# Attention heads of a fused float32 block: sixteen units turn their second head's probabilities on VectorE and through HBM, and use them a step later

## The chip, the cores and the metric

The kernel runs as one program on one core of a Trainium2 chip. The metric is the device time of one execution in microseconds (us), as the median of several runs. A profiled execution of the same program gives the trace from which all rows below are taken.

## What is computed

The reference is one layer on 512 tokens of width 1024, all in float32:

```python
x = x + cross_attention(layernorm(x), ctx, mask)      # 8192 context rows, width 1024
x = x + self_attention(layernorm(x))                  # 16 heads of 64, 4 key/value heads
x = x + expert_ffn(layernorm(x))                      # 16 experts, top 2, and a shared part
```

The change is nearly all in the second line. For each group of heads it computes, with causal masking, RMS-normed and rotated q and k:

```python
scores = einsum('bkgtd,bksd->bkgts', qg, k) * scale
attn = softmax(where(causal, scores, -inf), axis=-1)
y = einsum('bkgts,bksd->bkgtd', attn, v)
y_out = y - sum(y * vn) * vn                          # vn: v at unit length
out = y_out @ Wproj + y_out @ p_A @ p_B
```

## The kernel before

**Stages.** Layer norm and projections of the cross-attention come first, then the loop over the context in 8 pairs of chunks, then the self-attention, then the experts. Large products are made of three passes each (high times high, low times high, high times low), which are the matmuls of lines 37, 38 and 39. In the trace's names `banks` is PSUM.

**The loop over the context.** A pair of chunks has 7 products of two tiles each (`product`), whose scores VectorE takes with the mask (`scored`, line 1693, and `hold`, line 1676). ScalarE's `exps` makes the probabilities, VectorE's `turn` (line 1709) transposes each 32x32 block of them, SyncE stores the tile to HBM (`store_turned`, line 800) and fetches it back in four DMAs with the blocks in their places (`load_turned`, line 808), and ScalarE and VectorE split it into a high and a low part (`pt_hi`, line 1381, and `pt_lo`). `keys_hi` and `keys_lo` split the keys. Each engine's order is written out by hand; the change touches `first_half`, that of the first pair. There TensorE may begin the product numbered 3 when `added` has reached 3, which is the first `hold`, and its second tile at 4, which is the second `hold`.

**The self-attention.** There are 32 units: a tile of 128 queries and a pair of heads. Units 0 to 7 see 512 keys, 8 to 15 see 384, 16 to 23 see 256 and 24 to 31 see 128. A step `st` of the loop does on each engine, in this order:

- TensorE: the scores of unit st (line 1205), the transposes of the probabilities of unit st-1, both heads (line 1218), the values of unit st-2 (line 1234), and in between parts of the projections of later pieces (`fill`, lines 37 to 39), which have nothing to do with these units. At some half steps (`slot`) it also turns a piece or a row of outputs.
- ScalarE: at some steps the copy of a projected piece (line 1533); the copy of the first head's transposed probabilities of unit st-1 out of PSUM (`pt_act`, line 1568), then the exponentials of unit st (`exps`, line 1577), then at some steps squares of a piece; a turned piece is copied at its slot (line 1561).
- VectorE: causal mask and row maxima of unit st (lines 1930 and 1934), the copy of the second head's transposed probabilities of unit st-1 (`pt_dve`, line 1942), `row_recip`, the taking of the values of unit st-2 (line 1952), and work on the pieces.
- GpSimd: small products of the outputs, and DMAs: the output weights (`load_output_weights`, line 952), tables.
- SyncE: before the loop's first step it has issued `clear_rows` (line 778), one DMA of zeros into `y_dram`, and then it waits until all pieces are turned, to load the first shared expert weights (line 884).

`s_exp`, `pt_ready`, `pt_act`, `pt_dve`, `y_ready` and `y_done` count these operations; a buffer of transposed probabilities, `pT_sb`, holds two units.

Of the kernel before, what the change touches and what calls it, by code (L numbers as in the profile page):

```python
# [7 lines left out]
F32 = mybir.dt.float32  # L8
# [3 lines left out]
ACT = mybir.ActivationFunctionType  # L12
AX = mybir.AxisListType

P = 128
# [4 lines left out]
W = 512  # L20
# [500 lines left out]
H, HKV, HD = 16, 4, 64  # L521
# [14 lines left out]
HALVES_SPLIT = 15  # L536
TILE_OF = (2, 3, 0, 1, 0, 1, 2, 3)
PT_RING = 8
Y_BANK, FILL_BANK = 4, 5
MINC = 10  # L540
MAXC = (2 * T - 16) // P + 16
# [23 lines left out]
def attention(nc, block, m, ins, resid, QT, K, V, X, raw, PT, at, in_loaded, raw_loaded, ident, y_cleared, ln, d, F, weff,  # L565
# [28 lines left out]
    with ExitStack() as stage:  # L594
# [162 lines left out]
        def keys_of(u):  # L757
            return (SEQ[u // PAIRS] + 1) * P

        def s_banks(u):  # L760
            return bank[:, 2:4, :] if u % 2 == 0 else bank[:, 6:8, :]

# [19 lines left out]
        def _(sp):  # L782
# [29 lines left out]
            def pair_of_chunks(s_):  # L812
# [74 lines left out]
        def _(pool):  # L887
# [115 lines left out]
            root(6)  # L1003
            turn_by_sin(6)
            for st in range(3, UNITS + 4):
                if st % 2 == 0 and st >= 4:
                    part_along((st - 4) // 2)
                if st % 2 and (st - 3) // 2 < 4 * HKV:
                    times_value((st - 3) // 2)
# [23 lines left out]
        def _(pe):  # L1033
# [175 lines left out]
            def heads_transpose(u):  # L1209
                pe.wait_ge(s["s_exp"], u + 1)  # L1210
                if u >= 1:
                    pe.wait_ge(s["pt_act"], u)
                    pe.wait_ge(s["pt_dve"], u)
# [8 lines left out]
            def heads_values(u):  # L1222
                g = 2 * (u % PAIRS) // GROUP
                pe.wait_ge(s["pt_act"], u + 1)
                pe.wait_ge(s["pt_dve"], u + 1)
                if u == 0:
                    pe.wait_ge(s["piece_copied"], AHEAD)
                k = 2 * (u + 2)
                if not slot_read(pe, k) and not slot_read(pe, k - 1) and u >= 1:
                    pe.wait_ge(s["y_done"], u)  # L1230
                keys = keys_of(u) // P
                for h in range(2):
                    for k in range(keys):
                        mm = pe.matmul(bank[:, Y_BANK, h * HD:(h + 1) * HD],  # L1234
                                       pT_sb[:, u % 2, h, k * P:(k + 1) * P], v_sb[:, k, g * HD:(g + 1) * HD],
                                       start=k == 0, stop=k == keys - 1)
                mm.then_inc(s["y_ready"], 1)

# [9 lines left out]
            def slot(k):  # L1248

                if k not in PIECE_SLOTS.values() and k not in ROWS_SLOTS.values():  # L1250
                    return
                step = k // 2
                if k % 2 or not slot_read(pe, k - 1):
                    if step - 1 - (k % 2 == 0) >= 1:
                        pe.wait_ge(s["y_done"], step - 1 - (k % 2 == 0))
# [91 lines left out]
        def _(act):  # L1347
# [61 lines left out]
            def first_half():  # L1409
                keys_hi(2)  # L1410
                keys_hi(3)
                copy_first(0, 0)
                copy_first(0, 1)
                keys_hi(4)
                keys_hi(5)
                exps(0)
                keys_hi(6)
                exps(1)
                keys_hi(7)
                keys_hi(8)  # L1420
                keys_hi(9)
                pt_hi(0)
# [140 lines left out]
            def pt_act(u):  # L1563
                n = keys_of(u)
                act.wait_ge(s["pt_ready"], u + 1)
                if u >= 2:
                    act.wait_ge(s["y_ready"], u - 1)
                act.activation(pT_sb[:, u % 2, 0, 0:n], bank[:, 0, 0:n], ACT.Copy).then_inc(s["pt_act"], 1)

            def exps(u):  # L1570
                n = keys_of(u)
                act.wait_ge(s["s_max"], u + 1)
                if u >= 2:
                    act.wait_ge(s["pt_ready"], u - 1)
                    act.wait_ge(s["recip_done"], u - 1)
                for h in range(2):
                    op = act.activation(p_sb[:, u % 2, h, 0:n], s_banks(u)[:, h, 0:n], ACT.Exp,
                                        bias=s_neg_max[:, u % 2, h:h + 1], accum_out=s_rowsum[:, u % 2, h:h + 1])
                op.then_inc(s["s_exp"], 1)

# [74 lines left out]
        def _(dve):  # L1655
# [117 lines left out]
            def first_half():  # L1773
# [163 lines left out]
            def pt_dve(u):  # L1937
                n = keys_of(u)
                dve.wait_ge(s["pt_ready"], u + 1)
                if u >= 2:  # L1940
                    dve.wait_ge(s["y_ready"], u - 1)
                dve.tensor_copy(pT_sb[:, u % 2, 1, 0:n], bank[:, 1, 0:n]).then_inc(s["pt_dve"], 1)

            def row_recip(u):
                dve.wait_ge(s["s_exp"], u + 1)
# [96 lines left out]
            for st in range(UNITS + 2):  # L2042
                if st >= OUT_STEP + 3 and (st - OUT_STEP) % 3 == 0:
                    add_out((st - OUT_STEP - 3) // 3)
                slot(2 * st)
                if st < UNITS:
                    maxima(st)
                if 1 <= st <= UNITS:
                    pt_dve(st - 1)
                    row_recip(st - 1)  # L2050
                if st >= 2:
                    take_y(st - 2)
                if st >= 4 and st % 2 == 0:
                    dot((st - 4) // 2)
                if st >= 5 and st % 2 == 1:
                    take_along((st - 5) // 2)
                slot(2 * st + 1)
                if st == 0:
                    turn_by_cos(5)
# [1100 lines left out]
```

## Time and profile before

| | |
|---|---|
| median of 3 runs | 1351.06 us (1350.43 to 1351.42) |
| the profiled execution's own time | 1351.05 us |
| span of its trace | 1349.3 us |
| TensorE busy | 1326.9 us (98%) |
| VectorE, ScalarE busy | 927.6 us (69%), 719.2 us (53%) |

The span is the stretch from the first to the last instruction; 1.75 us of the execution's own time lie around it. Busy time of an engine is the union of its instructions; a matmul's end is modelled, so the length of a piece of TensorE's work is better read from start to start. In rows of the trace PE is TensorE, PEld its weight loads, DVE VectorE, ACT ScalarE, POOL GpSimd, SP SyncE.

### The profile page before, as it was taken

What the parts mean: (1) busy time and instruction counts of PE and PEld (TensorE: products, weight loads), DVE (VectorE), ACT (ScalarE), POOL (GpSimd) and SP (SyncE); (2) the same over time, 40 slices, a digit from 0 to 9 for tenths busy, and PEclk for the clock granted to TensorE, in tenths of its full rate; (3) what the DMA queues carried; (4) which work ended last, traced back from release to release, by engine and by line L of the source; (5) the groups of instructions that cost most, each with busy time, mean ns of one, the idle gap of its engine ahead of it and who ended that gap; (6) DMA issues with size and microseconds to landing.
All of it is one profiled execution on the core that took longest, in us unless ns stands there. A gap on an engine that the chain in (4) does not pass through costs nothing.

```text
span 1349.3 us, 17583 instructions
## 1 busy us (share of the span) xinstructions
PE 1326.9 (98%) x6228; PEld 1087.2 (81%) x6228; DVE 927.6 (69%) x1416; ACT 719.2 (53%) x1165; POOL 184.4 (14%) x244
## 2 busy tenths in 40 slices
PE   7999999999999999999999999999999999999999
PEld 5878878888888888888888888777777888888887
DVE  6757867675775857667675775867666676767665
ACT  3333446574665656656565653655433345667561
POOL 3000100000000000000000000634331022122113
PEclk9999999999999999999999999999999999999999
DMA  7457274674746748465575445503403357988676
GB/s 249 155 216 249 83 240 158 213 231 141 249 137 214 220 138 282 126 214 176 196 225 164 142 140 196 171 1 125 148 14 114 136 187 254 305 299 306 224 250 218
DMA packets 102887, 253.25 MB, mean 188 GB/s; under 512 B 10080, under 2 KB 56224, under 8 KB 89440
## 3 DMA queue, kind: packets, MB, share of 16 engines
q1 hardware_dynamic: 89136, 192.97, 43.6%
q0 software_dynamic: 10784, 48.93, 10.6%
q10 hardware_dynamic: 2880, 10.22, 1.9%
q8 instruction: 50, 0.82, 0.2%
q14 instruction: 37, 0.30, 0.1%
HBM read 210.67 MB, written 41.42 MB: 187 GB/s over the span
## 4 chain that ended last, share of the span: by engine, by line
PE 93%; DVE 3%; issue 1%; ACT 1%; DMA 1%; POOL 1%; SPq 0%; POOLq 0%; DVEq 0%; ACTq 0%
PE banks L37 25%; PE banks L39 25%; PE banks L38 25%; PE a_banks L37 3%; PE a_banks L38 3%; PE a_banks L39 3%; PE banks L1234 3%; PE banks L1205 2%; PE banks L1218 2%; DMA e_raw<-w_down 1%; PE banks L2444 1%; DVE e_lo L2778 0%; POOL c_ms L933 0%; DVE QT_lo L1873 0%; PE a_banks L273 0%
## 5 line engine op out<-in xcount | busy, mean ns | idle before, releaser
L37 PE MATMUL banks<-V_hi,b_PT_hi 128*128 128x512 f32 x512 | 199.3, 389 | 0.0
L38 PE MATMUL banks<-V_lo,b_PT_hi 128*128 128x512 f32 x512 | 199.2, 389 | 0.0
L39 PE MATMUL banks<-V_hi,b_PT_lo 128*128 128x512 f32 x512 | 199.2, 389 | 0.0
L1392 ACT ACTIVATE resid<-banks 128x1024 f32<-128x1024 f32 x64 | 65.5, 1023 | 104.0 <-PE banks L39 104.0
L2778 DVE TENSOR_TENSOR e_lo<-e_raw,e_hi 128x1024 fp32r<-128x1024 f32 x80 | 96.1, 1242 | 34.8 <-ACT e_hi L2605 34.1
L37 PEld LDWEIGHTS banks<-V_hi,b_PT_hi 128*128 128x128 f32 x512 | 96.1, 188 | 20.1 <-DVE V_lo L1663 0.2
L39 PEld LDWEIGHTS banks<-V_hi,b_PT_lo 128*128 128x128 f32 x512 | 96.1, 188 | 19.9
L38 PEld LDWEIGHTS banks<-V_lo,b_PT_hi 128*128 128x128 f32 x512 | 96.1, 188 | 19.9
L1693 DVE CUSTOM_DVE_ANT_0 b_s<-banks,b_s,b_row_max 128x512 f32<-128x512 f32 x60 | 45.0, 751 | 85.6 <-PE banks L39 85.6
L890 POOL DMA_DIRECT2D b_s<-mask x32 | 23.2, 726 | 575.8 <-DVE b_turned L1709 550.1
L37 PE MATMUL banks<-b_k_hi,QT_hi 128*128 128x512 f32 x256 | 99.6, 389 | 0.0
L38 PE MATMUL banks<-b_k_lo,QT_hi 128*128 128x512 f32 x256 | 99.6, 389 | 0.0
L39 PE MATMUL banks<-b_k_hi,QT_lo 128*128 128x512 f32 x256 | 99.6, 389 | 0.0
L2605 ACT ACTIVATE e_hi<-e_raw 128x1024 fp32r<-128x1024 f32 x80 | 81.7, 1061 | 29.2 <-DMA e_raw<-w_down 20.0
L1363 ACT ACTIVATE b_k_hi<-b_k_raw 128x1024 fp32r<-128x1024 f32 x60 | 61.6, 1049 | 38.8 <-DVE b_k_raw L1745 20.5
L37 PE MATMUL banks<-b_k_hi,b_q_hi 128*128 128x512 f32 x192 | 75.5, 393 | 2.5 <-DVE b_s L1676 2.5
L1658 DVE TENSOR_TENSOR b_k_lo<-b_k_raw,b_k_hi 128x1024 fp32r<-128x1024 f32 x60 | 71.7, 1220 | 5.5 <-ACT b_k_hi L1363 5.5
L39 PE MATMUL banks<-b_k_hi,b_q_lo 128*128 128x512 f32 x192 | 75.3, 392 | 0.0
L38 PE MATMUL banks<-b_k_lo,b_q_hi 128*128 128x512 f32 x192 | 75.3, 392 | 0.0
L1676 DVE TENSOR_TENSOR b_s<-banks,b_s 128x512 f32<-128x512 f32 x32 | 22.0, 691 | 77.1 <-PE banks L39 77.1
L1663 DVE TENSOR_TENSOR V_lo<-b_v_raw,V_hi 128x2048 fp32r<-128x2048 f32 x30 | 68.7, 2289 | 3.5 <-ACT V_hi L1372 3.5
L1398 ACT ACTIVATE banks<-resid,b_alpha 128x1024 f32<-128x1024 f32 x60 | 67.2, 1120 | 2.0
(364 smaller groups left out, 3236.7 us busy)
## 6 DMA issues: line engine op xcount, KB each, us to landing
b_v_raw<-kv SPq DMA_DIRECT2D x30, 1024.0 KB, 5.6
e_raw<-w_up SPq DMA_DIRECT2D x40, 512.0 KB, 5.2
e_raw<-w_down SPq DMA_DIRECT2D x40, 512.0 KB, 6.3
b_k_raw<-kv SPq DMA_DIRECT2D x19, 1024.0 KB, 5.5
raw<-kv SPq DMA_DIRECT2D x18, 1024.0 KB, 5.5
b_s<-mask POOLq DMA_DIRECT2D x32, 512.0 KB, 5.8
pt_dram<-b_turned SPq DMA_DIRECT2D x64, 256.0 KB, 3.3
b_p_in<-pt_dram SPq DMA_DIRECT2D x256, 64.0 KB, 4.2
```

Source lines behind the costliest of these rows:

```text
L37: pe.matmul(out, lhs_hi, rhs_hi, start=first, stop=False, skip_group_check=onto)
L38: pe.matmul(out, lhs_hi, rhs_lo, start=False, stop=False, skip_group_check=onto)
L39: return pe.matmul(out, lhs_lo, rhs_hi, start=False, stop=last, skip_group_check=onto)
L1234: mm = pe.matmul(bank[:, Y_BANK, h * HD:(h + 1) * HD], pT_sb[:, u % 2, h, k * P:(k + 1) * P], v_sb[:, k, g * HD:(g + 1) * HD], start=k == ...
L1363: act.activation(k_hi[:, j % 3, :, :], keys_raw(j), ACT.Copy).then_inc(hi_done, 1)
L1392: act.activation(resid[:, TILE_OF[n % PER_PAIR], :], O_ps(n), ACT.Copy).then_inc(b["acc_done"], 1)
L1398: act.activation(O_ps(n), resid[:, TILE_OF[c], :], ACT.Copy, scale=alpha[:, c:c + 1]).then_inc(b["seeded"], 1)
L1658: dve.tensor_tensor(k_lo[:, j % 3, :, :], keys_raw(j), f32(k_hi[:, j % 3, :, :]), ALU.subtract).then_inc(split_done, 1)
L1663: dve.tensor_tensor(value_slot(V_lo, vh), v_raw[:, :, :], f32(value_slot(V_hi, vh)), ALU.subtract).then_inc(b["v_split"], 1)
L1693: dve.tensor_tensor_reduce(slot, score_bank(s_, i, t), slot, 1.0, LEAST if n < TB else top_before, ALU.add, ALU.max, top).then_inc(b["adde ...
L2605: act.activation(e_hi(first + j), e_raw[:, j, :], ACT.Copy).then_inc(s["e_hi"], 1)
L2778: dve.tensor_tensor(e_lo[:, first + j, :], e_raw[:, j, :], f32(e_hi(first + j)), ALU.subtract).then_inc(s["e_split"], 1)
```

## The change

Units 0 to 15 (`MOVED`) no longer have their second head transposed on TensorE. `exps` writes that head's probabilities with their 32-column blocks in another order, VectorE transposes 32x32 blocks (`turn_probs`), SyncE stores the tile to HBM, waits for it and fetches it in four DMAs (`move_probs`), and ScalarE copies it into order (`keep_moved`). The values of these units are computed at step u+3 instead of u+2 (`LATE`), so step 18 has the values of units 15 and 16. What follows from the values (`take_y`, `times_value`, `dot`, `part_along`, `take_along`) follows a step later too, and two turns of output rows are moved from half steps 40 and 42 to 42 and 44. The loop's `clear_rows` comes behind the sixteen moves on SyncE. In the first pair of chunks `exps(1)` goes ahead of `keys_hi(6)`, `turn(0)` ahead of `keys_lo(6)`, and `hold(0, 0, 0)` ahead of `keys_lo(7)`.

```diff
+MOVED = 2 * PAIRS
+LATE = 1
-ROWS_SLOTS = {8: 28, 9: 30, 10: 40, 11: 42, 12: 56, 13: 58}
+ROWS_SLOTS = {8: 28, 9: 30, 10: 42, 11: 44, 12: 56, 13: 58}
+        p_turned, p_moved, p_kept = (at(f"c_p_{x}", [P, 2, W], F32, "raw", 4096 * i)
+                                      for i, x in enumerate(("turned", "moved", "kept")))
...
+        def kept(u, h):
+            return pT_sb[:, u % 4 // 2, u % 2, :] if u < MOVED else pT_sb[:, u % 2, h, :]
+        def values_at(st):
+            early = [st - 2 - LATE] if 0 <= st - 2 - LATE < MOVED else []
+            return early + ([st - 2] if MOVED <= st - 2 < UNITS else [])
...
@@ sync
+            def move_probs(u):
+                n, done = keys_of(u), STEPS // 2 + u // 2
+                sp.wait_ge(b["turned"], STEPS + u + 1)
+                sp.dma_start(pt_dram[u % PT_RING][:, 0:n], p_turned[:, u % 2, 0:n]).then_inc(b[f"pt_stored{u % 2}"], 16)
+                sp.wait_ge(b[f"pt_stored{u % 2}"], 16 * (done + 1))
+                if u >= 2:
+                    sp.wait_ge(b["pt_hi"], STEPS + u - 1)
+                for j in range(4):
+                    sp.dma_start(p_moved[32 * j:32 * j + 32, u % 2, 0:n].rearrange("p (a r) -> p a r", a=4),
+                                 pt_dram[u % PT_RING][:, 0:n].rearrange("(a i) (b r) -> b i a r", a=4, b=4)[j]
+                                 ).then_inc(pt_loaded[u % 2], 16)
...
+            for u in range(MOVED):
+                move_probs(u)
             clear_rows(sp)
@@ tensor
-                for h in range(2):
+                for h in range(1 if u < MOVED else 2):
                     for k in range(keys_of(u) // P):
                         mm = pe.transpose(bank[:, h, k * P:(k + 1) * P],
...
-                if st >= 2:
-                    heads_values(st - 2)
+                for u in values_at(st)[:1]:
+                    heads_values(u, st)
                 fill(st, 0)
+                for u in values_at(st)[1:]:
+                    heads_values(u, st)
@@ scalar, first_half
                 exps(0)
+                exps(1)
                 keys_hi(6)
-                exps(1)
@@ scalar
+            def keep_moved(u):
+                act.wait_ge(pt_loaded[u % 2], (16 if u % 2 == 0 else 0) + 64 * (STEPS // 2 + u // 2 + 1))
...
+                if 0 <= st - 2 - LATE < MOVED:
+                    keep_moved(st - 2 - LATE)
                 if 1 <= st <= UNITS:
                     pt_act(st - 1)
@@ vector, first_half
                 scored(1)
+                turn(0)
                 keys_lo(6)
-                turn(0)
-                keys_lo(7)
                 turn(1)
                 hold(0, 0, 0)
+                keys_lo(7)
                 hold(0, 0, 1)
@@ vector
+            def turn_probs(u):
+                dve.wait_ge(s["s_exp"], u + 1)
...
+                dve.transpose(p_turned[:, u % 2, 0:n], p_sb[:, u % 2, 1, 0:n]).then_inc(b["turned"], 1)
...
+                if 1 <= st <= MOVED:
+                    turn_probs(st - 1)
                 if st < UNITS:
                     maxima(st)
+                if MOVED < st <= UNITS:
+                    pt_dve(st - 1)
```

## Rows read from the trace of the kernel before

**Rows 1.** TensorE's wait in the first pair: us in total, times, longest.

```profile
PE banks L37 <- DVE b_s L1676: 2.5, 1, 2.5
```

**Rows 2.** Windows: length, busy us (instructions) of PE, PEld, DVE, ACT, POOL; clock; DMA share, GB/s.

```profile
864.60:908.00 43.40, 43.34 (x263) 32.17 (x263) 32.42 (x61) 24.01 (x93) 17.93 (x18) 1.00 0.00 1
908.00:948.00 40.00, 40.00 (x262) 31.06 (x261) 29.93 (x63) 21.28 (x79) 17.64 (x22) 1.00 0.28 106
```

**Rows 3.** Timeline of TensorE, a step with 512 keys, one with 384: start, us.

```profile
895.68 1.13 PE L1205 MATMUL banks<-c_kT,c_qT 64*128 64x512 f32 x4
896.74 1.09 PE L1218 MATMUL banks<-ident,c_probs 128*128 128x128 f32 x8
897.67 1.90 PE L1234 MATMUL banks<-c_v,c_PT 128*128 128x64 f32 x16
...
914.38 0.88 PE L1218 MATMUL banks<-ident,c_probs 128*128 128x128 f32 x6
915.09 1.90 PE L1234 MATMUL banks<-c_v,c_PT 128*128 128x64 f32 x16
```

**Rows 4.** The lines of block transpose, of copies; ns min/median/max, first and last start.

```profile
L1709 DVE STREAM_TRANSPOSE b_turned<-b_s x64: 702/703/710, 168.2 to 781.8; 128x512 f32<-128x512 f32 x64
...
L1942 DVE COPY c_PT<-banks x32: 280/482/681, 870.8 to 1012.1; 128x512 f32<-128x512 f32 x8, 128x384 f32<-128x384 f32 x8, 128x256 f32<-128x256 f32 x8, 128x128 f32<-128x128 f32 x8
...
L1381 ACT ACTIVATE b_PT_hi<-b_p_in x64: 611/616/635, 176.9 to 799.1; 128x512 fp32r<-128x512 f32 x64
```

**Rows 5.** Timeline of the second exponential of a 512-key and of a 384-key unit.

```profile
899.83 0.20 ACT L1577 ACTIVATION_READ_ACCUMULATOR c_probs<-banks,c_neg_max 128x1 f32 x1
...
916.99 0.20 ACT L1577 ACTIVATION_READ_ACCUMULATOR c_probs<-banks,c_neg_max 128x1 f32 x1
```

**Rows 6.** Timeline of SyncE's queue, first stores and loads of turned tiles.

```profile
168.90 2.12 SPq L800 DMA_DIRECT2D pt_dram<-b_turned  x2
171.06 3.85 SPq L808 DMA_DIRECT2D b_p_in<-pt_dram  x8
```

**Rows 7.** The page's DMA issues: KB each, median us to landing.

```profile
pt_dram<-b_turned SPq DMA_DIRECT2D x64, 256.0 KB, 3.3
b_p_in<-pt_dram SPq DMA_DIRECT2D x256, 64.0 KB, 4.2
```

**Rows 8.** Timeline, second and third step of the heads, VectorE, ScalarE, TensorE.

```profile
868.36 0.69 DVE L1888 TENSOR_TENSOR c_cosp<-c_piece,c_cos 128x512 f32<-128x512 f32 x1
...
873.73 0.43 DVE L1930 TENSOR_TENSOR banks<-banks,c_causal 128x256 f32<-128x256 f32 x1
...
875.45 0.69 ACT L1577 ACTIVATE c_probs<-banks,c_neg_max 128x512 f32<-128x512 f32 x1 [0.51 <-DVE c_neg_max L1934]
...
875.82 0.19 PEld L37 LDWEIGHTS banks<-K_hi,QT_hi 128*128 128x128 f32 x1
...
877.62 1.13 PE L1205 MATMUL banks<-c_kT,c_qT 64*128 64x512 f32 x4
877.72 0.60 ACT L1561 ACTIVATE c_qT<-banks 128x512 f32<-128x512 f32 x1 [0.83 <-PE banks L1163]
...
878.22 0.59 ACT L1533 ACTIVATE c_piece<-banks 128x512 f32<-128x512 f32 x1
```

**Rows 9.** A window behind the first pair's wait (columns as in rows 2).

```profile
173.00:174.00 1.00, 1.00 (x4) 0.81 (x3) 0.02 (x1) 0.00 (x0) 0.00 (x0) 0.50 0.83 168
```

**Rows 10.** Timeline of the first pair, ahead of that wait's end.

```profile
166.89 0.71 ACT L1406 ACTIVATE b_s<-b_s,b_neg_max 128x512 f32<-128x512 f32 x1
...
167.02 1.23 DVE L1658 TENSOR_TENSOR b_k_lo<-raw,b_k_hi 128x1024 fp32r<-128x1024 f32 x1 [0.88 <-ACT b_k_hi L1363]
...
170.61 1.28 DVE L1676 TENSOR_TENSOR b_s<-banks,b_s 128x512 f32<-128x512 f32 x2
```

**Rows 11.** Landings in the heads' stretch, and the zeros over the span.

```profile
K_lo<-weff_lo POOLq DMA_DIRECT2D x4, 1024.0 KB, 9.9
...
y_dram<-c_zeros SPq DMA_DIRECT2D x1, 6656.0 KB, 27.7
```

More of the change, by code:

```diff
@@ L758, in keys_of, with by_lanes, kept_free, values_through @@
             return (SEQ[u // PAIRS] + 1) * P
+        def by_lanes(x, n):
+            return x.rearrange("p (b k i) -> p k b i", b=4, k=n // P)
+        def kept(u, h):
+            return pT_sb[:, u % 4 // 2, u % 2, :] if u < MOVED else pT_sb[:, u % 2, h, :]
+        def kept_free(eng, u, h):
+            if u < MOVED:
+                if u >= 4:
+                    eng.wait_ge(s["y_ready"], u - 3)
+            elif u < MOVED + 2:
+                eng.wait_ge(s["y_ready"], MOVED - 3 + 2 * (u % 2) + h)
+            else:
+                eng.wait_ge(s["y_ready"], u - 1)
+        def values_at(st):
+            early = [st - 2 - LATE] if 0 <= st - 2 - LATE < MOVED else []
+            return early + ([st - 2] if MOVED <= st - 2 < UNITS else [])
+        def values_through(st):
+            return sum(len(values_at(i)) for i in range(st + 1))
+        def late_group(st, after):
+            q, odd = divmod(st - after - LATE, 2)
+            early = [q] if not odd and 0 <= q < MOVED // 2 else []
+            q, odd = divmod(st - after, 2)
+            return early + ([q] if not odd and MOVED // 2 <= q < UNITS // 2 else [])
         def s_banks(u):
@@ L1005, in _ @@
             for st in range(3, UNITS + 4):
[L1006 to L1009, printed above, removed]
+                for q in late_group(st, 4):
+                    part_along(q)
+                for q in late_group(st, 3):
+                    times_value(q)
                 if st in TAKEN:
@@ L1220, in heads_transpose, with heads_values @@
                 mm.then_inc(s["pt_ready"], 1)
-            def heads_values(u):
+            def heads_values(u, st):
                 g = 2 * (u % PAIRS) // GROUP
                 pe.wait_ge(s["pt_act"], u + 1)
-                pe.wait_ge(s["pt_dve"], u + 1)
+                if u < MOVED:
+                    pe.wait_ge(b["pt_hi"], STEPS + u + 1)
+                else:
+                    pe.wait_ge(s["pt_dve"], u - MOVED + 1)
                 if u == 0:
                     pe.wait_ge(s["piece_copied"], AHEAD)
-                k = 2 * (u + 2)
-                if not slot_read(pe, k) and not slot_read(pe, k - 1) and u >= 1:
+                k = 2 * st
+                if values_at(st)[0] != u:
+                    pe.wait_ge(s["y_done"], u)
+                elif not slot_read(pe, k) and not slot_read(pe, k - 1) and u >= 1:
                     pe.wait_ge(s["y_done"], u)
@@ L1233, in heads_values @@
                     for k in range(keys):
-                        mm = pe.matmul(bank[:, Y_BANK, h * HD:(h + 1) * HD],
-                                       pT_sb[:, u % 2, h, k * P:(k + 1) * P], v_sb[:, k, g * HD:(g + 1) * HD],
+                        if u < MOVED and h:
+                            left = p_kept[:, u % 2, k * P:(k + 1) * P]
+                        else:
+                            left = kept(u, h)[:, k * P:(k + 1) * P]
+                        mm = pe.matmul(bank[:, Y_BANK, h * HD:(h + 1) * HD], left, v_sb[:, k, g * HD:(g + 1) * HD],
                                        start=k == 0, stop=k == keys - 1)
@@ L1253, in slot @@
                 if k % 2 or not slot_read(pe, k - 1):
-                    if step - 1 - (k % 2 == 0) >= 1:
-                        pe.wait_ge(s["y_done"], step - 1 - (k % 2 == 0))
+                    if values_through(step - (k % 2 == 0)) >= 1:
+                        pe.wait_ge(s["y_done"], values_through(step - (k % 2 == 0)))
                 for i, at_slot in PIECE_SLOTS.items():
@@ L1565, in pt_act @@
                 act.wait_ge(s["pt_ready"], u + 1)
+                kept_free(act, u, 0)
+                act.activation(kept(u, 0)[:, 0:n], bank[:, 0, 0:n], ACT.Copy).then_inc(s["pt_act"], 1)
+            def keep_moved(u):
+                n = keys_of(u)
+                act.wait_ge(pt_loaded[u % 2], (16 if u % 2 == 0 else 0) + 64 * (STEPS // 2 + u // 2 + 1))
                 if u >= 2:
                     act.wait_ge(s["y_ready"], u - 1)
-                act.activation(pT_sb[:, u % 2, 0, 0:n], bank[:, 0, 0:n], ACT.Copy).then_inc(s["pt_act"], 1)
+                act.activation(p_kept[:, u % 2, 0:n].rearrange("p (k a j) -> p k a j", a=4, k=n // P),
+                               p_moved[:, u % 2, 0:n].rearrange("p (a k j) -> p k a j", a=4, k=n // P),
+                               ACT.Copy).then_inc(b["pt_hi"], 1)
             def exps(u):
@@ L1575, in exps @@
                     act.wait_ge(s["recip_done"], u - 1)
+                if 2 <= u < MOVED + 2:
+                    act.wait_ge(b["turned"], STEPS + u - 1)
                 for h in range(2):
-                    op = act.activation(p_sb[:, u % 2, h, 0:n], s_banks(u)[:, h, 0:n], ACT.Exp,
+                    to, of = p_sb[:, u % 2, h, 0:n], s_banks(u)[:, h, 0:n]
+                    if u < MOVED and h:
+                        to, of = by_lanes(to, n), of.rearrange("p (k b i) -> p k b i", b=4, k=n // P)
+                    op = act.activation(to, of, ACT.Exp,
                                         bias=s_neg_max[:, u % 2, h:h + 1], accum_out=s_rowsum[:, u % 2, h:h + 1])
@@ L1939, in pt_dve @@
                 dve.wait_ge(s["pt_ready"], u + 1)
+                kept_free(dve, u, 1)
+                dve.tensor_copy(kept(u, 1)[:, 0:n], bank[:, 1, 0:n]).then_inc(s["pt_dve"], 1)
+            def turn_probs(u):
+                n = keys_of(u)
+                dve.wait_ge(s["s_exp"], u + 1)
                 if u >= 2:
-                    dve.wait_ge(s["y_ready"], u - 1)
-                dve.tensor_copy(pT_sb[:, u % 2, 1, 0:n], bank[:, 1, 0:n]).then_inc(s["pt_dve"], 1)
+                    dve.wait_ge(b[f"pt_stored{u % 2}"], 16 * (STEPS // 2 + u // 2))
+                else:
+                    dve.wait_ge(s["w_split"], 6)
+                dve.transpose(p_turned[:, u % 2, 0:n], p_sb[:, u % 2, 1, 0:n]).then_inc(b["turned"], 1)
             def row_recip(u):
@@ L2045, in _ @@
                 slot(2 * st)
+                if 1 <= st <= MOVED:
+                    turn_probs(st - 1)
                 if st < UNITS:
                     maxima(st)
+                if MOVED < st <= UNITS:
+                    pt_dve(st - 1)
                 if 1 <= st <= UNITS:
-                    pt_dve(st - 1)
                     row_recip(st - 1)
[L2051 to L2056, printed above, removed]
+                for u in values_at(st):
+                    take_y(u)
+                for q in late_group(st, 4):
+                    dot(q)
+                for q in late_group(st, 5):
+                    take_along(q)
                 slot(2 * st + 1)
```

3 lines of the change are left out of this document (2 added, 1 removed).

## Prediction

> **What bounds the kernel now.** I read the busy shares first: TensorE is at work in 98% of the span, every other engine in 69% or less. The windows of the heads' stretch came next [rows 2]: TensorE is busy for 43.34 of 43.40 us while the units with 512 keys run, and for all of the 40.00 us of those with 384, at a granted clock of 1.00, the 2.4 GHz level. So a transpose taken off TensorE shortens this stretch, as long as nothing else takes its place. VectorE has 32.42 and 29.93 us of work there, ScalarE 24.01 and 21.28. The list of TensorE's waits gave the one place in the loop over the context where it stands still, 2.5 us for a `hold` in the first pair of chunks [rows 1]; behind it the clock falls to 0.50, the 1.2 GHz level [rows 9]. The timelines of the engines gave the rest.
>
> **The transposes.** From the first transpose to the first value matmul it is 897.67 - 896.74 = 0.93 us for eight, and 915.09 - 914.38 = 0.71 us for six [rows 3], so 0.11 us for each one more. Eight units lose four each (8 x 0.44 = 3.5 us) and eight lose three (8 x 0.33 = 2.6 us): **-6.2 us**. If each were worth its mean, 0.93 / 8 = 0.116, the 56 would give 6.5 us. The fill between is the same work.
>
> The Trainium skill, VectorE: DVE Perf Modes, section "Rules for kernel authors", speaks against the change: for a full 128x128 transpose it names TensorE where PSUM is an acceptable destination. That rule weighs one transpose by itself; in this trace VectorE's block transpose of 128x512 takes 0.703 us [rows 4], against 0.44 us of TensorE saved, and what decides is that TensorE is the full engine.
>
> **VectorE and ScalarE.** For the copy out of PSUM, 0.681 us at most, VectorE gets a block transpose of 0.703 us [rows 4]: nothing. ScalarE gets the copy into order as one more operation: the same kind of permuted copy takes 0.616 us [rows 4], 16 x 0.6 = 10 us in 83 us in which it is idle for 38. It covers this itself; what counts is where it stands, since `pt_act` and the next `exps` are queued behind its wait for the DMAs.
>
> **The round trip.** Scores of a 512-key unit start at 895.68 and its exponentials end at 900.03 [rows 3, 5], 4.35 us later. Turn, 0.70 us: 5.05. Then SyncE: a store issued at 168.90 has landed by the first load at 171.06, and the four loads are 1.9 us of issuing; the copy that waits for them begins at 176.9 [rows 4, 6], 8.0 us after the store. That gives 13.1 us, and 13.7 with ScalarE's copy. The values need it three steps later behind scores and transposes. A step is 43.4 / 8 = 5.4 us now [rows 2] and about 5.0 then: 15.0 + 1.06 + 0.5 = 16.5 us. Slack 2.8 us. With 384 keys: the last exponential of the unit whose transposes follow at 914.38 ends at 917.19 [rows 5], 3.7 us after its scores began 0.85 us ahead of those transposes; 0.5 + 8.0 + 0.5 more are 12.7 us, against 3 x 4.7 + 1.2 = 15.3. Slack 2.6 us. Where VectorE has 2 us of a piece's work ahead of the turn, about 0.6 is left. SyncE is busy with a unit for 2.16 + 1.9 = 4.1 us, less than a step. Its added waits, for the turn, the landing and `keep_moved` of unit u-2, hold up nothing but its own next units and the zeros; `exps(u)` also waits for the turn of unit u-2, which is a step old by then. The DMA engines are as good as idle until 908 us (0.00) [rows 2]. So in the quiet steps: nothing.
>
> **The start.** The values of unit 0 no longer fill step 2, while the first units' exponentials take as long as before. VectorE ends the piece's product at 869.05 [rows 8], turns unit 0 until 869.75, and comes to the maxima of unit 2 at 873.8 as before, but with a turn of 0.70 first: 874.5. From the mask to the exponentials it is 875.45 - 873.73 = 1.7 us [rows 8], and they take 1.45: 877.65. TensorE's transposes of unit 1 begin at 873.2 now (the fill behind them at 875.82 [rows 8], less 0.93 for them and 1.7 for the values) and at about 873.0 then, held by that unit's exponentials, until 873.5; then fill and a piece's turn, 877.62 - 875.82 = 1.8 us [rows 8], then scores, 1.06: 876.35. It waits 1.4 us for the exponentials of unit 2, transposes until 878.2, and then wants `keep_moved(0)`. ScalarE has a turned piece (0.5) and a piece's copy (0.6) ahead of it: 877.65 + 0.5 + 0.6 + 0.6 = 879.4. That is 1.2 us more: **+2.6 us**. The value work left out is done at step 18. Bounds: 1 us, if ScalarE's two copies come after or overlap, 4 if maxima slip once more or the clock falls.
>
> **Output weights and zeros.** GpSimd's 4 MB of output weights, twice, take about 10 us each until the last has landed [rows 11]. The first falls on about three moves of units 10 to 13. No row shows a move beside just these. Below: nothing. By the medians of the loop over the context, 3.3 and 4.2 us [rows 7] against 2.0 to 2.2 and some 3.5, a unit loses 2 us, of which its slack of 0.6 to 2.6 covers most, and SyncE falls 1.3 us behind a unit with 0.6 spare in each step: a stall of 0 to 2 us. I take **+0.6**, nearer to the quiet rows, since only one transfer competes; above, 4 us.
>
> The Trainium skill, DMA: Bandwidth & Descriptors, section "Queues, rings and completion order", has each DMA engine change between queues only after a whole packet of one; by this the small transfers wait behind the weights' packets, but a few, not the whole 4 MB. No row of this kernel shows it alone, and the term above doesn't use it.
>
> The zeros, 27.7 us long [rows 11], now start behind unit 15, at about 945 us, together with the second output weights. Those are needed some 12 us later, and 20 for the second half. Sharing may delay them by 0 to 4 us, most of it covered; **+0.2**. The shared weights land behind the zeros some 15 us later than now, and are first read after 1010.
>
> **The first pair.** With `exps(1)` (0.9 us) first, the key half that TensorE needs is split 1.1 us later: `keys_lo(6)` from 168.1 to 169.3 instead of 167.02 [rows 10], then a turn until 170.0 and the first `hold` until 170.6; today the two holds are at 170.61 to 171.89 [rows 10]. TensorE starts 0.65 us earlier, but its second tile wants the second `hold`, now behind `keys_lo(7)`, at 172.4: 0.45 us back. **-0.2 us**. The bounds: +0.5, and -2.4 if the shorter stretch of rest leaves the clock up: behind today's, some 3.4 us run at the 1.2 GHz level [rows 9], worth 1.7.
>
> **Sum.** -6.2 - 0.2 + 2.6 + 0.6 + 0.2 = -3.0 us, made against the profiled execution's 1351.05 us, which is the median of the runs to 0.01: **1348.1 us**.
>
> **Rivals.**
> 1. *The whole gain arrives.* The start's waits are covered, and the first pair keeps its clock: 1351.05 - 6.2 - 1.9 + 1.0 = 1344.0. For it: two of my terms are worked out to tenths from instruction starts. Against: no work is left to TensorE in step 2.
> 2. *Little is left.* The clock falls at the start, where TensorE now rests 2.6 us within 3.1, much as in the first pair: +1.7, or the weights cost 2 us more: 1349.5 to 1350. For it: rows 9. Against: the rest is in two pieces with transposes between.
> 3. *The move is too slow, and it ends slower.* SyncE takes the units one by one, so store, its landing and four issues bound the step. It decides from 4.7 us on. At the median landing of 3.3 us it is 3.3 + 0.1 + 1.9 = 5.3 us, over eight steps of 5.0 and eight of 4.7: 2.4 + 4.8 = 7.2 us lost: 1348.1 + 7.2 = 1355.3. For it: the median is of the same transfer. Against: that median has megabyte loads ahead in the same queue, and the heads' stretch has none.
>
> **Chances.** Forecast 0.43, little left 0.27, whole gain 0.13, too slow 0.17. 0.2% is 2.7 us, about what a measurement of this kernel can tell from no change, so the line lies at 1348.4, and the forecast case straddles it: faster 0.50 (0.37 of the forecast and the whole gain), same 0.31, slower 0.19. The likeliest case's own range is 1346.5 to 1349.3; over all cases 1343.8 to 1354.5.
>
> **What would show it.** TensorE waits of 1.4 and 1.2 us for the exponentials of unit 2 and for `keep_moved(0)`; 104 transposes in line 1218's place instead of 160; ScalarE's `keep_moved` seldom waiting for a DMA except at units 10 to 13; steps of about 5.0 and 4.7 us; the same 83 us of work 3 us shorter in all; in the first pair two waits of 1.8 and 0.4 us. Landings above 3 us in the quiet steps, or a wait of TensorE for ScalarE in every step, would make it wrong.

## The result, and the profile after

The changed kernel takes 1367.77 us (median of 4 runs, 1366.31 to 1369.51) against 1350.74 us of the kernel before (4 runs, 1348.37 to 1351.42): ratio 1.0132, interval 1.012 to 1.0144. It is 17 us slower, on the other side of no change and outside the range. The profiled execution took 1366.4 us, of which 1364.6 are span: 15.35 us over the profiled execution of before.

The sum of the forecast must have missed something of about 18 us, and something so large is seen in the list of TensorE's waits. Of the kernel after (us in total, times, longest):

```profile
PE banks L1292 <- ACT c_p_kept L1633: 7.7, 2, 6.8
PE banks L1292 <- issue: 5.9, 1, 5.9
PE banks L1292 <- DVE QT_lo L1947: 2.2, 5, 0.7
...
PE banks L37 <- DVE b_s L1750: 1.6, 1, 1.6
PE banks L1267 <- ACT c_probs L1649: 1.3, 1, 1.3
```

Line 1292 is the values (1234 before), line 1633 `keep_moved`, line 1267 the transposes. The value matmuls stand still twice, for 6.8 and 5.9 us; in the same list of before the values wait 0.7 us at most. The two waits forecast for the start are there too: 1.3 us for the exponentials, and 7.7 - 6.8 = 0.9 us for `keep_moved(0)`. The windows of the kernel after say where (columns as in rows 2). These go from the scores of unit 0 to those of units 8, 13 and 14, and on over the second place:

```profile
862.43:903.52 41.09, 38.92 (x220) 27.36 (x220) 31.38 (x60) 26.98 (x98) 17.19 (x18) 1.00 0.28 90
903.52:928.65 25.13, 25.13 (x158) 19.03 (x157) 18.21 (x39) 15.07 (x57) 11.65 (x15) 1.00 0.43 145
928.65:943.08 14.43, 7.63 (x30) 5.86 (x29) 3.98 (x8) 3.51 (x16) 3.93 (x5) 0.69 0.65 214
943.08:960.82 17.74, 17.56 (x111) 13.04 (x110) 11.89 (x28) 12.14 (x44) 5.47 (x9) 0.97 0.40 125
960.82:975.00 14.18, 8.32 (x35) 7.20 (x36) 1.82 (x6) 1.71 (x7) 2.58 (x3) 0.64 1.10 369
```

Until 928.65 all is about as forecast. Then step 13 takes 14.43 us where a step takes 4.6, and another 5.9 us are lost behind 960.82. In both places the clock is below 1.00. What TensorE waits for at 930.04 is read in the chain that ended last, of the kernel after (start, us):

```profile
920.76 1.86 DMA pt_dram<-c_p_turned
922.64 0.30 SPq L898
...
924.49 11.70 DMA c_p_moved<-pt_dram
936.22 0.53 ACT c_p_kept L1633
936.84 2.80 PE banks L1292 x12
```

The store of unit 10 lands in 1.86 us, its four loads in 11.70. What else was on its way shows only in GpSimd's own timeline of the kernel after, which the chain doesn't name:

```profile
921.46 0.64 POOL L1000 DMA_DIRECT2D K_hi<-weff_hi  x1
922.11 0.55 POOL L1000 DMA_DIRECT2D K_lo<-weff_lo  x1
922.65 0.54 POOL L1000 DMA_DIRECT2D K_hi<-weff_hi  x1
923.18 0.54 POOL L1000 DMA_DIRECT2D K_lo<-weff_lo  x1
```

These are the output weights, 1 MB each, issued just before and between the four loads of 48 KB. By the trace the weights landed at 926.8, 929.6, 932.5 and 935.9, and the loads, issued from 922.64 to 924.49, at 930.0, 932.9, 935.4 and 936.2. That looks like one line in order of issue, in which a load waits for all weights issued before it. But the third load, issued at 923.91, behind the last of the weights, landed half a microsecond before that one. The packets of the two queues, the pieces in which the DMA engines move a transfer, tell what happened. These are GpSimd's queue (q0) and SyncE's (q1) of the kernel after, from 924 to 927 us and from 927 to 930 (packets, MB, share of the 16 DMA engines' time):

```profile
q0 software_dynamic: 161, 1.19, 102.9%
q1 hardware_dynamic: 23, 0.01, 1.8%
```

```profile
q0 software_dynamic: 145, 1.06, 92.9%
q1 hardware_dynamic: 148, 0.05, 10.5%
```

From 927 us on the two queues alternate, one packet of the weights for one of the loads, and from 930 to 933 it is 145 and 143. The weights' packets carry 8 KB, the loads' 384 bytes. The eight megabytes of the output weights are 1152 packets, so 144 for each: 128 with data and 16 of a few bytes that end it. The four loads of unit 11, quiet ones, and the start of a store, from 937 to 939.5 us:

```profile
DMA packets 667, 0.34 MB, mean 135 GB/s; under 512 B 576, under 2 KB 667, under 8 KB 667
```

576 packets for four loads are 144 for each of 48 KB, as many as a megabyte of weights has. So while weights are under way, a load takes as long as a megabyte: 144 of its packets at 148 in 3 us are 2.9 us, and the second landed 2.9 us behind the first. Before that, from 922.7 to 926.4 us, SyncE's queue moved 4 packets and GpSimd's 173, though in a quiet step a load has landed after 2.0 us. What held the loads back there no run shows.

The second place is much the same with unit 15, whose loads are issued from 956.02 and the second four megabytes from 955.87: 156 packets of the weights and 158 of SyncE's queue from 961 to 964 us. Two summaries of the tile `c_p_moved` after show how rare this is, and so why a median says nothing of it:

```profile
L1633 ACT ACTIVATE c_p_kept<-c_p_moved x16: 514/572/645, 876.0 to 967.3; 128x512 f32<-128x512 f32 x8, 128x384 f32<-128x384 f32 x8
...
  DMA c_p_moved<-pt_dram: 12.5, 2
...
DMA to landing us min/median/max: 1.7/2.0/11.7
```

The stop costs more than its length. These windows of the kernel after take in the work from the end of either wait, 936.84 and 967.90, to where the clock comes back, and one of the work between the two places:

```profile
967.90:974.90 7.00, 7.00 (x27) 6.42 (x28) 0.68 (x3) 1.08 (x5) 0.73 (x1) 0.50 1.11 345
936.84:944.20 7.36, 7.36 (x26) 5.73 (x26) 2.89 (x6) 2.41 (x7) 2.52 (x3) 0.50 0.32 80
944.30:962.04 17.74, 17.56 (x114) 13.18 (x112) 11.92 (x30) 11.13 (x42) 6.08 (x10) 1.00 0.48 153
```

At 0.50, the 1.2 GHz level, 7.36 and 7.00 us of work would have been half as long: 3.7 and 3.5 us more lost.

**The account of the traces.** Two waits, 6.80 + 5.86 = 12.7 us; the clock behind them, 7.2; two waits at the start, 2.2; transposes, -6.2 as forecast. That is 15.9 us, and the two traces show 17.1 from the scores of unit 0 to those of unit 31 (1023.59 - 862.43 = 161.16 us after, 1008.71 - 864.66 = 144.05 before), so 1.2 us of the transposes' gain did not come. The scores of unit 0 themselves start 2.2 us earlier, and what follows unit 31 adds 0.4: 17.1 - 2.2 + 0.4 = 15.3.

### The profile page after: what moved, and what is told of

It reads as the page before. It is cut to its first block, busy times and chain, and to the rows that moved or that the text cites. A ratio compares the mean times of both kernels' runs of the same rounds, so it can differ in the third digit from the quotient of the medians.

```text
span 1364.6 us, 17612 instructions
## 1 busy us (share of the span) xinstructions
PE 1328.6 (97%) x6172; PEld 1086.8 (80%) x6172; DVE 925.7 (68%) x1416; ACT 726.4 (53%) x1181; POOL 185.7 (14%) x244
## 4 chain that ended last, share of the span: by engine, by line
PE 91%; DVE 3%; issue 2%; DMA 1%; POOL 1%; ACT 1%; SPq 0%; ACTq 0%; POOLq 0%; DVEq 0%
PE banks L37 25%; PE banks L39 24%; PE banks L38 24%; PE a_banks L37 3%; PE a_banks L38 3%; PE a_banks L39 3%; PE banks L1292 3%; PE banks L1253 1%; DMA c_p_moved<-pt_dram 1%; DVE resid L3108 1%; PE banks L1267 1%; PE banks L2529 1%; POOL c_ms L981 0%; DVE QT_lo L1947 0%; PE a_banks L273 0%
## 5 line engine op out<-in xcount | busy, mean ns | idle before, releaser
L37 PE MATMUL banks<-K_hi,QT_hi 128*128 128x512 f32 x160 | 67.9, 425 | 1.3 <-DVE QT_lo L1947 1.1
```

What stands on the lines that cost most here:

```text
L37: pe.matmul(out, lhs_hi, rhs_hi, start=first, stop=False, skip_group_check=onto)
```

## The experiments

Each was timed on one chip beside the kernel before, so the ratio counts more than the time. Diffs are against the kernel after, unless said.

**Fewer bytes, same issues.** Is it the weights at all?

```diff
-pool.dma_start(w_piece(x, w), parts[w - 6].rearrange("p (e n) -> p e n", n=W)
+pool.dma_start(w_piece(x, w)[:, 0:1, :], parts[w - 6].rearrange("p (e n) -> p e n", n=W)[:, 0:1, :]
```

> The changed kernel with a quarter of the output weights' bytes: each of the eight 1 MB DMAs behind line 1000 brings one of its four blocks only, so the last products of the self-attention use old values in the other blocks. Theory A (TensorE's waits of 6.8 and 5.9 us and the two stretches of 10.2 us at the 1.2 GHz level come from small transfers of a moved unit that land only with the 4 MB of output weights issued just ahead of them): both waits fall to at most 1 us each and the clock stays up, so 1367 less 12.7 less 10.2 is about 1344 to 1346 us. Theory B (SyncE takes the units one by one and falls behind the steps of 4.7 us by itself): waits for keep_moved stay, the time stays above 1360 us. Theory C (the zeros, now issued behind unit 15, delay what the later steps need): the wait at 962 us stays, the one at 930 us may go, about 1356 us.

Measured: 1354.92 us (4 runs, 1351.16 to 1358.15), ratio 1.0045 (1.0028 to 1.0062): 12.9 us of the 17 come back, but not the 21 to 23 that theory A forecast. The waits of the kernel with short weights:

```profile
PE banks L1292 <- issue: 2.4, 1, 2.4
...
PE banks L1292 <- ACT c_p_kept L1633: 1.5, 2, 0.9
```

The first place is down to 0.6 us (1.5 - 0.9), the second to 2.4, and behind that some 6.8 us still run at the 1.2 GHz level. It is the weights. But with a quarter of their bytes the loads still took up to 6.4 us, more than half of 11.7. The number of the weights' packets has not changed, they are 2 KB now in place of 8: from 926 to 928 us there are 286 of them, and 369 of SyncE's queue. So the price goes with the packets that alternate and with what each carries, not with the bytes alone.

**The first pair alone, and all but the first pair.** The first is the kernel before with the new order in `first_half`, the second the kernel after with the old one.

> The kernel before with the new order in the first pair of chunks alone. Theory A (what the trace of the changed kernel shows there: a wait of 1.65 instead of 2.49 us, no second one, and no stretch of 3.4 us at the 1.2 GHz level behind it): 0.8 + 1.7 = 2.5 us faster, 1348.2 us against 1350.7. Theory B (my forecast: 0.2 us faster, the clock falls as before): 1350.5 us.

> The changed kernel with the first pair of chunks in the order of before. If the parts add up, 2.2 us more than the changed kernel (what first_pair_only won): about 1370 us. If the clock's stretch at the 1.2 GHz level in the first pair falls in some executions only, 1368 to 1370.

Measured: 1347.74 us (12 runs), ratio 0.9988 (0.9979 to 0.9998), and 1368.73 us (4 runs), ratio 1.0139 (1.0124 to 1.0155). The part alone gives 1.6 us, and without it the whole is 1.0 us slower, within the intervals: small, and a gain. A window of 3 us behind the wait, of the kernel with the first pair alone; before had 0.50 here [rows 9]:

```profile
172.00:175.00 3.00, 2.97 (x13) 2.11 (x12) 2.12 (x3) 0.19 (x1) 0.00 (x0) 1.00 0.87 196
```

But the kernel with the old order, and its wait of 2.5 us, kept its clock there in its profile as well:

```profile
172.00:175.00 3.00, 2.71 (x12) 2.28 (x13) 1.87 (x3) 0.00 (x0) 0.54 (x1) 1.00 0.81 209
```

So 0.84 us (2.49 less 1.65) is the shorter wait, and how often the clock falls behind either order is open.

**Eight units.** The moves end before the weights are issued; half of the transposes' gain is given up.

```diff
-MOVED = 2 * PAIRS
+MOVED = PAIRS
```

> The changed kernel with MOVED = 8: only the units with 512 keys go through HBM, so no move is under way when the output weights are fetched. Theory A (collision with the output weights): no wait over 1.5 us but those at the start (1.3 and 0.9 us); 8 x 0.44 = 3.5 us of transposes saved, 2.2 us lost at the start, 2.5 us won in the first pair: 1350.7 - 3.8, about 1347 us. Theory B (SyncE's chain per unit is too slow): eight steps of 5 us leave it time, so about the same 1347; with short_weights the two theories come apart. Theory C (late zeros): the zeros now start about 910 us and meet the first output weights, so a wait at about 955 us for them, 1350 us or more.

Measured: 1349.03 us (10 runs), ratio 0.9993 (0.9984 to 1.0002). In the heads no wait over 0.7 us is left behind the start; the two of the start, 2.2 us, remain, and in this execution 3.4 us behind them run at 0.50, from 878.0. The long waits are gone although `clear_rows` now lies before the weights.

**The weights by another queue.** Is it GpSimd's queue, or the order of issue? The same loads come from ScalarE's queue.

```diff
+                if st == 11:
+                    act.wait_ge(weff_stored, 128)
+                    load_output_weights(6)
+                    load_output_weights(7)
+                if st == 16:
+                    load_output_weights(8)
+                    load_output_weights(9)
```

> The changed kernel with the eight DMAs of the output weights issued from ScalarE's queue, at its steps 11 and 16, instead of GpSimd's. Theory A (transfers are served in order of issue across queues): the moves issued behind them land with them again, waits of about 6 us at two places, about 1367 us. Theory B (GpSimd's queue alone is served ahead of SyncE's): the moves land in 2 to 4 us, waits under 1.5 us, about 1350 us.

Measured: 1367.29 us (2 runs), ratio 1.0129 (1.0107 to 1.0151), as the kernel after. ScalarE's timeline, then SyncE's, with the weights from ScalarE:

```profile
922.18 0.35 ACTq L1681 DMA_DIRECT2D K_hi<-weff_hi  x1
...
923.52 0.77 ACTq L1681 DMA_DIRECT2D K_lo<-weff_lo  x1
```

```profile
922.68 2.05 SPq L898 DMA_DIRECT2D c_p_moved<-pt_dram  x4
924.77 0.49 SPq L893 DMA_DIRECT2D pt_dram<-c_p_turned  x1
936.31 0.78 SPq L898 DMA_DIRECT2D c_p_moved<-pt_dram  x2
```

The next loads come at 936.31, when the store issued at 924.77 has landed: 11.5 us, against 1.9 in a quiet step; it stands behind its own queue's four loads. With two waits of 6.4 us in place of 6.8 and 5.9, and one of 1.8 at 957.2, it makes no difference which of the two queues has the weights. Theory B is refuted, but theory A is not shown by it: queues that alternate give the same time. The packets decide, ScalarE's queue (q10) and SyncE's in this kernel from 928 to 931 us:

```profile
q10 hardware_dynamic: 153, 1.12, 95.5%
q1 hardware_dynamic: 152, 0.05, 8.5%
```

Again it is one for one. Served in order of issue, the weights would have gone in a block.

**The weights by SyncE, one megabyte behind each store.** Within one queue the order can be chosen.

```diff
@@ move_probs, behind the store
+                if u >= 12:
+                    load_output_half(6 + (u - 12) // 2, u % 2)
@@ behind the loop of moves
+            for w in (8, 9):
+                for part in range(2):
+                    load_output_half(w, part)
```

> The changed kernel with the output weights' DMAs issued by SyncE: one of 1 MB right behind the store of each of units 12 to 15, ahead of the wait for that store, and the other four behind unit 15's loads, ahead of the zeros. Theory A (transfers are served in the order in which they are issued, whichever queue they are in): a store is never behind weights of its own unit, loads are behind at most 1 MB less the store's own 2 us, so each unit is up to 1.5 us later, SyncE falls behind by about 1 us per unit, and TensorE waits 0 to 3 us in all with the clock up: 1345 to 1349 us. If instead one queue or another is served first whatever the order of issue, the loads wait for the weights again and the time stays over 1355 us.

Measured: 1350.42 us (10 runs), ratio 1.0009 (0.9999 to 1.002). All 16 units are moved, and nearly all of the loss is gone; the time is 1.4 us above theory A's range. It doesn't tell the theories apart either, since weights and moves are now in one queue. Waits of 0.6 us at 930.6 and of 1.6 at 948.7 remain, the second with 3.4 us at the 1.2 GHz level behind it.

**Half megabytes, and the start.** From the kernel just told, pieces of 512 KB behind loads as well as stores. At the start the maxima of unit 2 go ahead of the turn of unit 1, and `keep_moved(0)` ahead of a piece's copy.

> The changed kernel with the output weights issued by SyncE in DMAs of 0.5 MB: one behind the loads of each of units 11 to 14 and one behind the store of each of units 12 to 15, the other eight behind unit 15's loads; and at the start the maxima of unit 2 ahead of unit 1's turn on VectorE, and keep_moved(0) ahead of the piece's copy on ScalarE. If order of issue decides: the wait of 1.58 us at step 17 and the 3.4 us at half clock behind it go (3.2 us), those at the start fall from 2.1 to 0.9 us: 1350.4 - 3.2 - 1.2, about 1346 us. If SyncE's unit chain is too full (4.1 us and a half megabyte each way in steps of 4.5 us), step 17 still waits 1 to 2 us and it stays at 1348 to 1350.

Measured: 1351.47 us (12 runs), ratio 1.0011 (1.0002 to 1.0019): a miss. The start's waits shrink to 0.7 and 0.4 us, 1.1 less, but SyncE's timeline in this kernel shows what the pieces cost:

```profile
928.20 0.38 SPq L912 DMA_DIRECT2D K_hi<-weff_hi  x1
928.62 0.43 SPq L893 DMA_DIRECT2D pt_dram<-c_p_turned  x1
...
933.60 1.75 SPq L900 DMA_DIRECT2D c_p_moved<-pt_dram  x4
...
935.86 0.43 SPq L893 DMA_DIRECT2D pt_dram<-c_p_turned  x1
```

From the store at 928.62 to the loads at 933.60 it is 5.0 us, where a quiet store takes 1.9. A unit takes SyncE 935.86 - 928.62 = 7.2 us against a step of 4.6; after four such units TensorE waits 2.8 us at 948.1, and 6.8 us run at the 1.2 GHz level. This is the third rival of the prediction, met only where weights stand ahead of the store.

**Only the second collision taken away.** GpSimd issues the second four megabytes when unit 15's loads have landed.

```diff
+                    pool.wait_ge(pt_loaded[1], 64 * (STEPS // 2 + 15 // 2 + 1))
```

> The changed kernel with one wait added on GpSimd: the second four DMAs of output weights are issued only when unit 15's loads have landed. The first four are left as they are. Theory A (each collision by itself costs its wait and the time at the 1.2 GHz level behind it, 5.9 + 5.1 us for the second): 1367.8 - 11.0 = 1356.8, up to 1358.8 if the later weights delay the output products by 2 us. Theory C (the zeros behind unit 15 are what hurts at step 18): no change, 1367.

Measured: 1359.73 us (4 runs), ratio 1.007 (1.0055 to 1.0086): 8.0 us less than the kernel after. The waits, with the second weights held:

```profile
PE banks L1293 <- ACT c_p_kept L1634: 7.6, 2, 6.7
```

The first wait of 6.7 us stays (7.6 less 0.9 at the start), the second is gone. The gain is less than expected. The second place is worth 5.9 + 3.5 = 9.4 us by the account, and the two traces bear that out: step 18 takes 5.82 us in place of 14.95, 9.1 less. With the later weights the steps 20 and 21 are 0.25 and 0.21 us longer (4.88 and 6.02). The rest is the clock in this execution: it fell for 3.4 us behind the start's waits too (step 3: 9.57 us in place of 7.97), and behind the first place for 6.8 us, not 10.2 (step 13: 13.58 in place of 14.43).

**Eight units with the mended start.** The kernel with eight units, and:

```diff
@@ scalar
+                if st == 3:
+                    keep_moved(0)
...
-                if 0 <= st - 2 - LATE < MOVED:
+                if 0 < st - 2 - LATE < MOVED:
@@ vector
-                if 1 <= st <= MOVED:
+                if 1 <= st <= MOVED and st != 2:
...
+                if st == 2:
+                    turn_probs(1)
```

> moved8 with the two changes at the start alone. Theory A (the start's waits of 1.28 and 0.88 us are VectorE's turn ahead of unit 2's maxima and ScalarE's piece copy ahead of keep_moved(0)): they fall to about 0.6 and 0.3 us, and the 3.4 us at the 1.2 GHz level behind them (1.7 us) go: 1349.0 - 1.3 - 1.7, 1346 to 1348 us. Theory B (the waits are the chain from scores to exponentials itself): no change, 1349.

Measured: 1346.36 us (9 runs), ratio 0.9977 (0.9968 to 0.9987): the fastest of all, 0.23% below before. About half of that need not be the heads': the first pair's order alone gave 0.9988 (0.9979 to 0.9998), and 0.9977 beside it lies within the intervals. Windows over the two places of the weights, and the landings of the moves:

```profile
904.00:929.00 25.00, 25.00 (x167) 20.02 (x166) 15.77 (x38) 13.43 (x48) 9.82 (x14) 1.00 0.89 249
929.00:944.00 15.00, 15.00 (x101) 11.49 (x99) 11.91 (x26) 9.18 (x35) 6.91 (x8) 1.00 0.99 357
```

```profile
DMA to landing us min/median/max: 1.8/1.9/2.3
```

The DMA engines are busier here from 904 to 944 us than in the kernel after (0.89 and 0.99 against 0.43 and 0.65 there), and TensorE never stands still: not the traffic hurts, but a short transfer beside it that someone waits for.

**Twelve units, weights behind the last of their loads.** From the kernel with eight: `MOVED = 12`, the zeros ahead of the moves, and GpSimd waits for unit 11's loads, at step 12 in one kernel and 13 in the other.

> moved8_start with 12 units moved, the zeros issued ahead of the moves as in the kernel before, and the first output weights issued only when unit 11's loads have landed. If order of issue is all that made the moves late: no wait over 0.7 us between steps 4 and 18, four more units save 3 x 0.11 each, 1.3 us, of which up to 0.7 goes into waits for the shared bank that the transposes had covered: 1345 to 1346 us against 1346.4 of moved8_start. If the later output weights are late at step 17, 1347 or more.

> moved12 with the first output weights issued by GpSimd a step later, behind its step 13. In moved12 GpSimd's four DMA issues stood ahead of its share of a piece, and VectorE's cosine product beside them took 2.36 us instead of 0.69; TensorE waited 1.5 us for a row turn behind it, and 13.7 us at the 1.2 GHz level followed. Theory A (that collision is all that was wrong with moved12): no wait over 0.7 us between steps 4 and 18, 1345 to 1346 us. Theory B (the steps of 4.5 us leave the clock so near its lower level that any small wait drops it): the executions spread over several us again, median 1348 to 1351.

Measured: 1350.96 us (11 runs, 1346.64 to 1355.18), ratio 1.0006 (0.9992 to 1.0021), and 1347.36 us (11 runs), ratio 0.998 (0.9971 to 0.9989); both forecasts were 1345 to 1346. The profiled execution of the first had a new wait of 1.5 us at 935.36 and the clock at 0.50 for 13.6 us behind it. Its timeline, TensorE, VectorE and GpSimd:

```profile
933.52 0.66 POOL L1023 TENSOR_TENSOR c_along<-c_vn,c_dots 128x256 f32<-128x256 f32 x1
...
933.75 2.36 DVE L1965 TENSOR_TENSOR c_cosp<-c_piece,c_cos 128x512 f32<-128x512 f32 x1
934.16 1.40 POOL L990 TENSOR_TENSOR c_sq<-c_piece,c_sin 128x256 f32<-128x256 f32 x2
...
936.03 0.68 DVE L1950 TENSOR_TENSOR QT_lo<-banks,QT_hi 128x512 fp32r<-128x512 f32 x1
...
936.86 0.85 PE L1293 MATMUL banks<-c_v,c_PT 128*128 128x64 f32 x6 [1.50 <-DVE QT_lo L1950]
```

The product with the cosines takes 2.36 us where it takes 0.69 [rows 8], while GpSimd works beside it; `QT_lo` comes late, and the values want its bank. That is one instance: elsewhere in this kernel, at 885.64, the same product takes 0.69 us while GpSimd does the same work from 885.69. There VectorE began first, here GpSimd was already at work; whether that is the difference wasn't tested. With the weights a step later it is gone. Twelve units on time are no better than eight (0.998 and 0.9977): four more units save 4 x 0.33 = 1.3 us, which neither interval could show.

## Why the prediction was wrong, step by step

**The step that failed** is the term "Output weights and zeros": +0.6 us, bounds 0 to 4. It measured 12.7 us of waits and 7.2 of clock, about 20 us. It named the right place, the moves of units 10 to 13, and the right cause, four megabytes beside small transfers. It sized it by medians, "3.3 and 4.2 us [rows 7] against 2.0 to 2.2", and took a value near the quiet rows, "since only one transfer competes". And of the rule that it cited it took the small transfers to wait behind the weights' packets, "but a few". The runs show that they are not few: the queues alternate packet for packet, and a load of 48 KB has 144 packets, as a megabyte of weights has, so four loads last as long as four megabytes, 7.4 to 11.7 us from issue to landing. The median of another stretch is the cost of what usually ran there, not an upper bound for four megabytes at once. The upper bound was in the rows: one whole landing of the weights, about 10 us [rows 11], less the slack of 2.6 us is 7.4 us, at each of the two places; 6.8 and 5.9 were measured. The second place was not seen at all: unit 15's loads and the second four megabytes are issued within 0.2 us of each other.

**The clock** stood only at the start and in the first pair. With a wait of 7 us as the bound it would have belonged here as well.

The Trainium skill's rule cited there (DMA: Bandwidth & Descriptors, "Queues, rings and completion order": an engine changes between queues after a packet) was taken for small costs, and left out of the sum. The trace agrees with the rule, with 145 packets of the one queue and 148 of the other in 3 us; what was wrong is how many packets a small transfer was taken to have. The first 3.7 us, in which SyncE's queue moved 4 packets to the other's 173, that doesn't explain.

**The transposes** were right with 512 keys: 0.11 us each. Before, from the scores of unit 4 to those of unit 9:

```profile
883.56 1.13 PE L1205 MATMUL banks<-c_kT,c_qT 64*128 64x512 f32 x4
...
913.53 0.92 PE L1205 MATMUL banks<-c_kT,c_qT 64*128 64x384 f32 x4
```

and after:

```profile
880.80 1.13 PE L1253 MATMUL banks<-c_kT,c_qT 64*128 64x512 f32 x4
...
908.59 0.92 PE L1253 MATMUL banks<-c_kT,c_qT 64*128 64x384 f32 x4
```

That is 29.97 us and 27.79, 0.44 less a step. With 384 keys two steps became 0.32 and 0.26 shorter, and steps 9 and 10 together hardly (20.70 us before and 20.06 after from unit 9's to unit 13's scores, -0.6 for -1.3). That is 0.7 of the 1.2 us that did not come. At such steps TensorE also turns a piece, in a bank that it shares with the values, and waits there for `QT_lo`; that this wait, covered by transposes before, took the gain is argued, not shown: the list of waits has 2.2 us for it against 2.0.

**The start**: +2.6 forecast in two waits of 1.4 and 1.2 (the first is 1.3 by the prediction's own numbers, 877.65 - 876.35), measured 1.28 and 0.88, 2.2 in all. Right, and both made smaller by order alone, to 0.7 and 0.4. VectorE and ScalarE: no cost in quiet steps, right.

**The round trip** in quiet steps was shorter than taken: store and loads land in 2.0 us each at the median, not 3.3 and more. The rival of a SyncE too slow was refuted for these; it holds only behind bulk. The prediction's range over all cases, up to 1354.5, left out that rival's own 1355.3.

**The first pair**: the wait of 1.65 us as forecast (1.8), the second of 0.45 absent; 1.6 us gained for 0.2, between the bounds. 0.84 us of it is the shorter wait; the rest is not shown.

**The zeros** hurt nothing that was seen: with eight units they overlap the weights, and those are still in time.

## What to carry to other kernels

Before a short DMA round trip is put on a path with a few microseconds of slack, list the issues of every engine in the stretch, and bound the landing by what else is under way on any queue, not by a median. Count the packets of the small transfer, too: each may have to wait for one of the bulk. Moving the bulk from GpSimd's queue to ScalarE's didn't help; issuing it behind the short transfers did, and so did moving only the units that come earlier. Whether loads of fewer packets would help, no run shows. And a wait of TensorE of several microseconds is to be priced with about half as much again for the clock behind it; a shorter one can cost more than its own length, as 2.8 us did with 6.8 us at the 1.2 GHz level.

## What the runs showed of the hardware

- Two queues with work alternated packet for packet: 145 and 148 in 3 us for GpSimd's and SyncE's, 153 and 152 for ScalarE's and SyncE's, though the packets were of 8 KB and of 384 bytes. So 48 KB took as long as 1 MB. Before that, SyncE's queue moved 4 packets in 3.7 us, and GpSimd's 173.
- Within SyncE's own queue, 512 KB ahead (and the four loads before them) made a store land in 4.3 to 5.0 us in place of 1.9.
- The 1.2 GHz level lasted 10.2 us from within each long wait of the kernel after, 6.8 us from within the same first wait of 6.7 us with the second weights held, and once 13.6 us behind a wait of 1.5 us; behind 1.65 us in the first pair it didn't come, and behind 2.5 us it came in one execution and not in another.
- A product on VectorE took 2.36 us in place of 0.69 beside GpSimd's in one place, and 0.69 beside the same work in another. Only the times were seen; the cause wasn't tested.
